# Two more comparisons behind each float-to-integer cast, in a transformer layer with quantised activations

## The reference

```python
def _quant_act(x):
    scale = 127.0 / jnp.clip(jnp.max(jnp.abs(x), axis=-1, keepdims=True), EPS, None)
    xq = jnp.clip(jnp.round(x * scale), -128.0, 127.0) / scale
    return x + jax.lax.stop_gradient(xq - x)

def _bitlinear(x, w):
    return jnp.einsum('bsi,oi->bso', _quant_act(x), _quant_weight(w))

h = jax.nn.gelu(_bitlinear(x, w1), approximate=False)   # in: 1024, out: 4096
y = _bitlinear(h, w2)                                   # in: 4096, out: 1024
x = x + attention(layernorm(x))
x = x + ffn(layernorm(x))       # _quant_act runs on layernorm(x) and on h
```

## Time and profile before

| What | us |
|---|---|
| Median of the timed runs (2) | 9252.16 |
| Lowest and highest | 9245.48, 9258.83 |
| The profiled execution | 9235.27 |
| Its span, from the first to the last instruction of the slowest core (core 4) | 9233.7 |
| Spans of the eight cores | 9174.2 to 9233.7 |
| Mean granted TensorE clock of the cores, as a share of full speed | 0.598 to 0.603 |

### The profile page before, as it was taken

How to read it: one execution, slowest core, us unless ns; L and a number is a source line. 1 busy time by engine, 2 the same in 40 slices (tenths; PEclk the granted TensorE clock), 3 DMA queues, 4 the chain that set the end, 5 groups by cost and what they waited for, 6 DMA issues and landing times.

```text
span 9233.7 us, 59243 instructions; the slowest of 8 cores (9174.2 to 9233.7 us)
## 1 busy us (share of the span) xinstructions
PE 4163.4 (45%) x19332; PEld 1639.2 (18%) x19456; DVE 2869.6 (31%) x4721; ACT 1928.0 (21%) x2129; POOL 0.2 (0%) x4
## 2 busy tenths in 40 slices
PE   4224555666665355566666530033333332024445
PEld 0000211222222121122222210011111111012222
DVE  0432232111111223211111127765555555650000
ACT  1012202443433220234444311100000000001111
POOL 0000000000000000000000000000000000000000
PEclk8676755555555575555555555566666666567778
DMA  4232000000000100000000010011111111112221
GB/s 156 100 120 87 21 0 0 1 1 1 1 1 21 66 24 0 0 1 1 1 1 1 21 59 34 32 37 55 55 55 55 55 55 55 46 66 73 73 73 53
DMA packets 199064, 358.67 MB, mean 39 GB/s; under 512 B 23257, under 2 KB 154718, under 8 KB 194674
## 3 DMA queue, kind: packets, MB, share of 16 engines
q1 hardware_dynamic: 198770, 354.87, 11.4%
HBM read 279.29 MB, written 75.50 MB: 38 GB/s over the span
## 4 chain that ended last, share of the span: by engine, by line
PE 40%; DVE 28%; ACT 14%; issue 8%; DMA 5%; SPq 3%; DVEq 1%; ACTq 0%
ACT pslab L763 6%; PE ps_PV L773 6%; PE ps_S L752 6%; PE ps_F L1195 5%; PE ps_F L1075 5%; PE pss L265 3%; PE ps_qn L730 3%; PE ps_W L830 2%; DVE htile L1122 2%; DVE htile L1123 2%; PE ps_mu L606 2%; DVE colmisc L1106 2%; DVE ao_tm L785 1%; PE ps_rs L610 1%; PE ps_trH L1134 1%
## 5 line engine op out<-in xcount | busy, mean ns | idle before, releaser
L752 PE MATMUL ps_S<-qt,kt 65*128 65x512 bf16 x2048 | 984.5, 610 | 279.4 <-ACT pslab L763 243.0
L763 ACT ACTIVATE pslab<-ps_S 128x1024 bf16<-128x1024 f32 x1024 | 994.7, 1022 | 152.1 <-PE ps_S L752 150.3
L1195 PE MATMUL ps_F<-hqin,w2tb 128*128 128x512 bf16 x2002 | 487.1, 402 | 555.9 <-DMA hqin<-scr_hq 382.6
L773 PE MATMUL ps_PV<-vaug,pslab 128*128 128x65 bf16 x8192 | 531.4, 242 | 457.3 <-DVE ao_tm L785 369.5
L783 DVE RECIPROCAL colmisc<-ps_PV 128x1 f32<-128x1 f32 x512 | 86.3, 169 | 1950.4 <-PE ps_PV L773 1950.4
L1134 PE MATMUL ps_trH<-s_idb,hqtm 128*128 128x128 bf16 x1024 | 129.4, 305 | 1201.7 <-DVE colmisc L1127 1100.0
L773 PEld LDWEIGHTS ps_PV<-vaug,pslab 128*128 128x128 bf16 x8192 | 462.9, 129 | 573.3 <-issue 573.3
L265 PE MATMUL pss<-wab,s_onescolf 128*1 128x512 f32 x512 | 308.0, 751 | 543.4 <-ACT wab L245 325.1
L1075 PE MATMUL ps_F<-w1tb,yi_fm 128*128 128x512 bf16 x2000 | 458.8, 389 | 184.5 <-DMA w1tb<-scr_w1t 181.0
L1099 ACT ACT_TABLE_LOAD x32 | 41.1, 1283 | 1792.7 <-DVE htile L1088 912.1
L1195 PEld LDWEIGHTS ps_F<-hqin,w2tb 128*128 128x128 bf16 x2048 | 210.8, 103 | 812.0 <-issue 607.1
(11 more groups left out here) (180 smaller groups left out, 4522.8 us busy)
## 6 DMA issues: line engine op xcount, KB each, us to landing
w1tb<-scr_w1t SPq DMA_DIRECT2D x512, 128.0 KB, 2.4
wst<-w1t SPq DMA_DIRECT2D x24, 2048.0 KB, 9.2
wst<-w2t SPq DMA_DIRECT2D x96, 512.0 KB, 3.3
xstage<-x SPq DMA_DIRECT2D x64, 512.0 KB, 3.3
scr_hq<-hqfm SPq DMA_DIRECT2D x256, 128.0 KB, 2.0
hqin<-scr_hq SPq DMA_DIRECT2D x256, 128.0 KB
scr_x<-x2asm SPq DMA_DIRECT2D x32, 512.0 KB, 2.9
f_xst<-scr_x SPq DMA_DIRECT2D x32, 512.0 KB, 3.2
```

The lines of the kernel that those rows point to most:

```text
L752: ins = q.matmul(out=psS[kt % 2][:, 512 * s:512 * (s + 1)], lhsT=kt65[:, N * g + 128 * kt: N * g + 128 * (kt + 1)], rhs=qt65[hb][:, 1024 * ...
L763: sA.inc(q.activation(out=pslab[:, 1024 * kt:1024 * (kt + 1)], in_=psS[kt % 2][:], func=AF.Exp))
L773: ins = q.matmul(out=psPV[:], lhsT=pslab[:, 1024 * kc + 128 * qt: 1024 * kc + 128 * (qt + 1)], rhs=vaug[:, 1040 * g + 65 * kc: 1040 * g + ...
L1195: ins = q.matmul(out=psF[:, half:half + 512], lhsT=w2tb[:, 1024 * hc + 128 * dc: 1024 * hc + 128 * (dc + 1)], rhs=hqin[:, 512 * hc:512 * ( ...
```

## The change

In both roundings the one comparison becomes three. With d the difference between the value and its cast, the cast value now gets one added for d > 0.5, one for d > 1.5 and one for d >= -0.5, and 129 is subtracted instead of 128. The running sum is kept in the buffer of the cast-back value (`yjunk`, `hflt`), while the difference stays in `ytmp` and in the slice of `htile`. The lines behind the edits move down by 4 in the second norm and by up to 8 behind the second one.

```diff
@@ ln3_quant_phase @@
                 VS(q, q.tensor_tensor(out=ytmp[:], in0=ytmp[:], in1=yjunk[:, 0:D],
                                       op=OP.subtract))
-                VS(q, q.scalar_tensor_tensor(out=ytmp[:], in0=ytmp[:], scalar=0.5,
+                VS(q, q.scalar_tensor_tensor(out=yjunk[:, 0:D], in0=ytmp[:], scalar=0.5,
                                              in1=yjunk[:, 0:D], op0=OP.is_gt, op1=OP.add))
-                sV.inc(q.tensor_scalar(out=yib[:, D * (t % 2):D * (t % 2 + 1)], in0=ytmp[:],
-                                       scalar1=128.0, scalar2=None, op0=OP.subtract))
+                VS(q, q.scalar_tensor_tensor(out=yjunk[:, 0:D], in0=ytmp[:], scalar=1.5,
+                                             in1=yjunk[:, 0:D], op0=OP.is_gt, op1=OP.add))
+                VS(q, q.scalar_tensor_tensor(out=yjunk[:, 0:D], in0=ytmp[:], scalar=-0.5,
+                                             in1=yjunk[:, 0:D], op0=OP.is_ge, op1=OP.add))
+                sV.inc(q.tensor_scalar(out=yib[:, D * (t % 2):D * (t % 2 + 1)], in0=yjunk[:, 0:D],
+                                       scalar1=129.0, scalar2=None, op0=OP.subtract))
@@ ffn1_phase @@
                         VS(q, q.tensor_tensor(out=hs, in0=hs, in1=hflt[:], op=OP.subtract))
-                        VS(q, q.scalar_tensor_tensor(out=hs, in0=hs, scalar=0.5,
+                        VS(q, q.scalar_tensor_tensor(out=hflt[:], in0=hs, scalar=0.5,
                                                      in1=hflt[:], op0=OP.is_gt, op1=OP.add))
-                        VS(q, q.tensor_scalar(out=hqtm[:, 1024 * sl:1024 * (sl + 1)], in0=hs,
-                                              scalar1=128.0, scalar2=None, op0=OP.subtract))
+                        VS(q, q.scalar_tensor_tensor(out=hflt[:], in0=hs, scalar=1.5,
+                                                     in1=hflt[:], op0=OP.is_gt, op1=OP.add))
+                        VS(q, q.scalar_tensor_tensor(out=hflt[:], in0=hs, scalar=-0.5,
+                                                     in1=hflt[:], op0=OP.is_ge, op1=OP.add))
+                        VS(q, q.tensor_scalar(out=hqtm[:, 1024 * sl:1024 * (sl + 1)], in0=hflt[:],
+                                              scalar1=129.0, scalar2=None, op0=OP.subtract))
```

## The result

| | before | after |
|---|---|---|
| Median of the timed runs, us | 9245.89 (8 runs, 9226.59 to 9258.83) | 9661.15 (9 runs, 9653.54 to 9718.12) |
| Profiled execution, us | 9235.27 | 9672.45 |
| Its span, us | 9233.7 | 9670.9 |

The ratio is 1.0459, with a 95% interval of 1.044 to 1.0477: the kernel is 4.6% slower, some 424 us (407 to 441); the two medians as they stand differ by 415. The forecast was +427 us and 9679, in a range of 9648 to 9710.

What follows compares the result with a forecast made beforehand. VectorE's quantisation sequences were taken to bound the two edited stages, with no slack inside them. 341.2 us (FFN) plus 85.8 (second norm) gave 427.0, so 9679.2 us against the timed median of 9252.16; range 9648 to 9710.

Steps and rivals of the forecast that it cites:

- What bounds the stages: Second norm and first FFN stage: while VectorE quantises, nothing else may work; TensorE's waits of 493.1 and 1100.0 us grow.
- steps 1 and 2: Both roundings: 64 plus 256, together 320 added VectorE instructions, at 1225 ns (second norm) and 1226 ns (FFN) each.
- The upper end for the new form: Both roundings: is_ge could cost up to 1285 ns instead of 1225, adding 19 us over 320 instructions.
- step 3: Both roundings: idle time with each added instruction, 0.107 us in the FFN stage and 0.116 us in the second norm.
- Second norm: Second-norm stage: 64 added instructions, each with its duration and gap, cost 85.8 us.
- FFN stage: First FFN stage: 256 added instructions, each with its duration and gap, cost 341.2 us.
- The sum: Whole kernel: both stages' costs together, 427.0 us, 4.6% of the time, giving 9679.2 us against the timed runs.
- The clock: TensorE's clock, despite longer idling ahead of the transposes, adds zero; 24 us if the slow part of the matmuls doubled.
- The price by rule: Added VectorE instructions by the skill's cycle table: 1127 ns each, an estimated 395 us in all; the trace's 1225 was preferred.
- Cheaper instructions: Both roundings: new instructions run at the one-input rate of 694 ns, adding 256 us, 9508 us; chance 0.02.
- dearer steps: Both roundings: each dependent instruction has a gap of 0.5 instead of 0.11 us, another 125 us, 9804 us; chance 0.03.
- Work that falls into idle time: Both stages: new instructions fill VectorE's 157 and 887 us of idle time, kernel stays at 9252 us; chance 0.02.

Runs made afterwards that it cites:

- e3_one_ge: The changed kernel with two of the three comparisons taken out in both places, leaving only the is_ge one with -0.5; ratio to the kernel before 0.9998.
- e8_interleave: The changed kernel with a row tile's 28 first-FFN-stage instructions reordered, two slices alternating with an `hflt` each, fewer waits for the instruction just ahead; 9529.32 us.
- e1_norm_only: The kernel before with the change made in the second norm alone (64 added instructions); ratio to the kernel before 1.0091.
- e2_ffn_only: The kernel before with the change made in the first FFN stage alone (256 added instructions); ratio to the kernel before 1.0368.
- e5_mm_512: The kernel before plus 256 useless 128x512 SCALAR_TENSOR_TENSOR in the FFN stage's matmul part, one behind each copy out of PSUM; ratio to before 1.0006.
- e6_mm_1024: The kernel before plus 256 useless 128x1024 SCALAR_TENSOR_TENSOR in the FFN stage's matmul part, one behind each copy out of PSUM; ratio to before 1.0073.

## Why the prediction was right

- **What bounds the stages** was right. TensorE's wait grew as it was named, by 339.1 and 86.4 us for the 341 and 86 forecast, and VectorE's own waits stayed. One reading was loose: it put the rest of VectorE's idle time in the FFN stage, 273 us, between the transpose rounds. 173.1 us of it lie there; 69 are the short gaps ahead of the five lines of the sequence itself (13.5 to 14.0 us each). They are part of the chain and not room in it, so the sum is not touched.
- **Count and duration** (steps 1 and 2) were right: 320 instructions at 1225 to 1226 ns. The upper end for the new form, 1285 ns, was not needed; e3_one_ge shows the old form's 1226 ns for the new one.
- **The gap** (step 3) was right in size, 0.107 us ahead of the three lines of the FFN stage and 0.103 to 0.116 in the second norm. What it is made of I had not asked; e8_interleave shows it as a wait of 0.19 us, of which 0.08 is hidden in the duration of the instruction ahead. For this change, which waits behind every instruction, the sum is the same.
- **The terms.** Second norm: forecast 85.8, measured 85.4 in the stage and 84 us by e1_norm_only. FFN stage: forecast 341.2, measured 337.3 in the stage, 343.1 in a second profile of the same kernel, and 340 us by e2_ffn_only. The 5.8 us between the two profiles are not in the quantisation, for TensorE's wait for it is 1439.1 us in both; VectorE's wait for the matmuls is 449.3 in one and 455.1 in the other.
- **The sum**, 427.0, against 424 us by the ratio, inside its interval of 407 to 441. The forecast of 9679 is 18 us above the measured median. That is not a term of the change: 9679 stood on the median of the two runs shown, and eight runs of before give 9245.89, 6 us lower; the other 12 are the difference between 427 and the medians' 415, within the interval of the ratio.
- **The clock** was right at zero: in the second block it is 0.96 for 0.95 in the matmul stretch and 0.51 for 0.51 in the quantisation. The Trainium skill, TensorE: Matmul & The Clock Gate, "Why this matters for your kernels", warns of idle gaps between bursts of matmuls. In this block the longer gaps took nothing more, as these rows show.
- **The price by rule.** The Trainium skill, VectorE: DVE Perf Modes, "The TRN2 errata", has a cycle table by which the sum would have been an estimated 395 us, below the measured interval. Its form for a two-input addition, 151 cycles and one per element, gives 1224 ns, and the rows have 1225 to 1226.
- **The rivals.** Cheaper instructions (9508 us) and dearer steps (9804) are out by the rows of after. Work that falls into idle time is out in this place by e1 and e2, and e5_mm_512 and e6_mm_1024 show it at work in the matmul part of the same stage: all of 174.4 us hidden there, and three quarters of 311.1. The rival named the right quantity, slack at the place, and the waits had put it at none.

## What to carry to other kernels

Price an added instruction by the nearest row of the same kind, with the gap behind it, and then ask the waits, not the busy share, whether the engine has slack at that place: VectorE here was idle for two thirds of the time, and all of 320 instructions were paid. An instruction of the same kind beside the matmuls of the same block is free up to the 0.98 us that each step leaves: the one of 0.68 us was, and of the one of 1.22 us only 0.33 us were paid. Where an engine's own chain is the path, count first (a rounding in two instructions gave back 7.3%), then let independent instructions alternate so that each waits for the one before the last.

## What the hardware did that I had not expected

- A wait for the instruction just ahead costs VectorE 0.19 us at 128x1024 in e8_interleave, for a two-input instruction (1.33 to 1.14 us) and for a cast (0.80 to 0.60 us) alike. The profile shows only 0.11 of it as idle time, because an instruction that doesn't wait starts some 0.08 us before the end recorded for the one ahead.
- The part ahead of the second norm, the same program in all of these kernels, ends between 5488 and 5517 us in the mean of the cores, and between 5465 and 5530 in single cores. The whole effect of the second norm's edit is only three times the spread of these means, so a difference of stages, marked by SyncE's first loads, is the sharper measure: the unedited second norm came out at 504.1 to 505.1 us in five kernels.
